# A megakernel on one Trainium2 core: two reorderings on ScalarE, two key copies moved to DMAs, paired maxima, a later projection and PE fillers

## What is computed

```python
# 1: window attention, 8 x 8 windows, 8 heads of 8 channels, rotary q and k
q, k, v = split(xw @ qkv_w.T + qkv_b); q, k = rope2(q), rope2(k)
h = softmax(q * 8 ** -0.5 @ k.T) @ v @ proj_w.T + proj_b
# 2: selective state-space block on layernorm(h), 4096 positions per image, 128 channels, 16 states
xb, z = split(rmsnorm(x) @ in_proj_w.T)
xb = silu(causal_conv4(xb) + conv_b)
delta = softplus(xb @ projDelta_w.T + projDelta_b)
B, C = xb @ projB_w.T, xb @ projC_w.T
s[t] = exp(delta[t] * A) * s[t-1] + xb[t] * delta[t] * B[t]      # 128 x 16 states
h = h + (sum(s * C) + xb * D) * silu(z) @ out_proj_w.T + x       # x is layernorm(h)
# 3: mixture of 6 experts, top 2, on layernorm(h)
w = softmax(top2(softmax(relu(f @ rw1 + rb1) @ rw2 + rb2)))
h = h + sum_e w_e * (relu(relu(f @ w1_e + b1_e) @ w2_e + b2_e) @ w3_e + b3_e)
```

## Time and profile before

| | |
|---|---|
| median of 3 runs | 1665.36 us (1664.95 to 1667.06) |
| the profiled execution's own time | 1668.21 us |
| its span, first to last instruction | 1666.4 us |
| first scan, last scan | 171.5 us, 1599.0 us |
| granted TensorE clock, mean | 0.828 of 2.4 GHz |
| HBM traffic | 274.75 MB read, 20.97 MB written |

### The profile page before, as it was taken

The page is one execution under the profiler, slowest core; times in us unless marked ns, Lnnn a source line. Parts: engine busy times, 40 slices in busy tenths (PEclk is TensorE's granted clock), DMA queues, the critical chain, the costliest instruction groups (busy, mean ns, idle before and its releaser), DMA issues. The chain is left out here.

```text
span 1666.4 us, 25330 instructions
## 1 busy us (share of the span) xinstructions
PE 1186.7 (71%) x7764; PEld 540.7 (32%) x7828; DVE 1251.3 (75%) x1453; ACT 1041.3 (62%) x1973; POOL 1089.3 (65%) x1475
## 2 busy tenths in 40 slices
PE   3665758696868678686968676786869687767565
PEld 1442425151524324151514233241515242212121
DVE  1112787797979788897979697887879797979841
ACT  2335757667585857676675858576776857564521
POOL 2014686777767686777767676777777677777630
PEclk9967968898888889798888888897988887676755
DMA  2002887686868778677868677687768687978720
GB/s 70 6 8 63 217 237 196 193 225 172 230 174 228 183 213 211 194 208 193 224 171 234 175 225 192 205 216 195 207 183 233 173 229 188 252 183 256 214 54 7
DMA packets 205982, 301.62 MB, mean 181 GB/s; under 512 B 70220, under 2 KB 70424, under 8 KB 205720
## 3 DMA queue, kind: packets, MB, share of 16 engines
q1 hardware_dynamic: 205848, 299.99, 66.1%
HBM read 274.75 MB, written 20.97 MB: 177 GB/s over the span
## 5 line engine op out<-in xcount | busy, mean ns | idle before, releaser
L1262 POOL TENSOR_TENSOR hc<-hs,c_rep 128x512 f32<-128x512 f32 x512 | 650.1, 1273 | 244.6 <-DVE hs L1035 244.5
L1035 DVE TENSOR_TENSOR_SCAN hs<-bank,state,xd 128x512 f32<-128x512 f32 x512 | 645.0, 1272 | 63.0 <-issue 44.2
L775 ACT ACTIVATE bank<-dl,a_neg 128x512 f32<-128x512 f32 x512 | 350.8, 688 | 242.1 <-DVE hs L1035 239.1
L1025 DVE TENSOR_TENSOR xd<-xd,bank 128x1024 f32<-128x1024 f32 x256 | 305.8, 1194 | 13.2 <-PE bank L423 7.7
L438 PE MATMUL bank<-hc,wts 128*32 128x512 f32 x1024 | 183.6, 779 | 3.3 <-POOL hc L1262 2.0
L543 PE MATMUL bank<-q_diag,k_heads 128*128 128x128 f32 x1024 | 155.1, 301 | 18.8 <-issue 8.6
L543 PEld LDWEIGHTS bank<-q_diag,k_heads 128*128 128x128 f32 x1024 | 156.3, 218 | 10.9 <-issue 5.0
L1055 DVE TENSOR_REDUCE neg_max<-bank 128x8 f32<-128x512 f32 x128 | 85.7, 675 | 74.3 <-PE bank L531 74.3
L531 PE MATMUL bank<-k_heads,q_diag 64*64 64x512 f32 x512 | 82.2, 715 | 73.2 <-DVE neg_max L1055 43.6
L702 PE MATMUL bank<-e,wts 64*64 64x512 f32 x384 | 70.2, 807 | 86.5 <-ACT e L961 86.5
L599 PE MATMUL bank<-xz,wts 128*128 128x512 f32 x128 | 77.1, 686 | 42.2 <-ACT xz L877 22.0
(11 more groups left out here) (167 smaller groups left out, 2021.2 us busy)
## 6 DMA issues: line engine op xcount, KB each, us to landing
xd<-xdel_rows SPq DMA_DIRECT2D x512, 256.0 KB, 4.5
dl<-delta_rows SPq DMA_DIRECT2D x512, 256.0 KB, 4.1
delta_rows<-delta SPq DMA_DIRECT2D x16, 512.0 KB, 2.9
xdel_rows<-xdel SPq DMA_DIRECT2D x16, 512.0 KB, 3.0
xin<-in_x_dram SPq DMA_DIRECT2D x32, 128.0 KB, 3.0
q_diag<-rot SPq DMA_DIRECT2D x64, 64.0 KB, 3.8
out_dram<-res SPq DMA_DIRECT2D x256, 16.0 KB
wts<-in_packed_dram SPq DMA_DIRECT2D x1, 1528.5 KB, 6.6
```

Of the source, the lines that this page charges most:

```text
L775: act.activation(decay_ps[n % 2][:, :], dl[:, n % 4, :], ACT.Exp, scale=a_neg[:, g:g + 1])\
L1025: dve.tensor_tensor(pair, pair, b_ps[:, :].unsqueeze(1).to_broadcast([128, 2, BAND]), ALU.mult)\
L1035: dve.tensor_tensor_scan(hs[:, n % 4, :], decay_ps[n % 2][:, :], xd[:, n % 8, :], state[:, g:g + 1], ALU.mult, ALU.add).then_inc(scanned.s ...
L1262: pool.tensor_tensor(hc[:, n % 8, :], hs[:, n % 4, :], c_rep[:, BAND * h:BAND * h + BAND], ALU.mult)\
```

## The change

- ACT: Silu with its table loads (slot 9) and Exp and Ln of softplus (slot 13) move into `soften`, called right behind the decay and the values' evacuation in the slot.
- Heads 6 and 7 of `k_heads` are written by 4 DMAs of 16 KB on SP's queue in slot 13, ahead of the queries' in slot 14. ACT copies heads 0 to 5, in slots s = 6 to 8; it has none at s = 5.
- Banks 4 and 5 become one tensor, `both`, and DVE takes the maxima of two windows in one instruction at s = 11, 13, 15, 17. A semaphore of its own, `maxed`, replaces the banks' drained counts for it; PE waits on it ahead of the scores of windows 2, 4, 6 and ahead of the transpose of the maxima.
- The projection's matmul goes from slot 10 to slot 11, ahead of the slot's other matmuls of the experts and of the preparation.
- `keep_busy` issues 3, 3, 3 and 2 bf16 matmuls (zero weights, 512 columns, accumulated into the y bank) at the start of slots 13, 14, 16 and 17.
- The output bias of slot 25 is one matmul of 128 columns instead of two of 64.

```diff
--- before.py
+++ after.py
@@ -81,11 +81,11 @@
-AT = {"S": [10, 12, 14, 16], "max": [10 + _w for _w in range(NW)],
+AT = {"S": [10, 12, 14, 16], "max": [11, 13, 15, 17],
       "T": [19, 20, 22, 23, 25, 26, 28, 29], "P": [21, 21, 24, 24, 27, 27, 30, 30]}
-FILLERS = {}
+FILLERS = {13: 3, 14: 3, 16: 3, 17: 2}
 SOFT = (15, 16, 17, 18, 19, 20, 21, 22)
@@ -104,19 +104,19 @@
 class Use:
-    def __init__(self, bank, filled, drained, index):
-        self.bank, self.index = bank, index
+    def __init__(self, bank, filled, drained, index, before):
+        self.bank, self.index, self.before = bank, index, before
         self.fills, self.drains = filled, drained
         self.filled, self.drained = filled.sem, drained.sem
     def opens(self, chunk):
-        return self.drains.at(chunk, self.index)
+        return self.drains.at(chunk, self.before)
     def full(self, chunk):
         return self.fills.at(chunk, self.index + 1)
     def empty(self, chunk):
-        return self.drains.at(chunk, self.index + 1)
+        return self.drains.at(chunk, self.before + 1)
 def tower(nc, x, packed, select, out):
@@ -130,17 +130,27 @@
         def sig(name, per):
             return Signal(sem(name), per)
-        psum = [ctx.enter_context(nc.psum_tensor(f"bank{i}", [128, 512], F32)) for i in range(8)]
+        psum = [ctx.enter_context(nc.psum_tensor(f"bank{i}", [128, 512], F32)) for i in range(4)]
+        both = ctx.enter_context(nc.psum_tensor("both", [128, 2, 512], F32))
+        psum += [both[:, 0, :], both[:, 1, :]]
+        psum += [ctx.enter_context(nc.psum_tensor(f"bank{i}", [128, 512], F32)) for i in range(6, 8)]
         decay_ps, b_ps, y_ps = psum[0:2], psum[2], psum[3]
-        def bank_uses(stage, uses, first):
-            count = [sum(b == bank for _, b in uses) for bank in range(max(b for _, b in uses) + 1)]
-            signals = [(Signal(sem(f"{stage}_filled{b}"), n), Signal(sem(f"{stage}_drained{b}"), n))
-                       for b, n in enumerate(count)]
-            return {name: Use(psum[first + b], *signals[b], [n for n, x in uses if x == b].index(name))
-                    for name, b in uses}
-
-        A = bank_uses("a", A_USES, 4)
+        def bank_uses(stage, uses, first, apart=()):
+
+            names = [[n for n, b in uses if b == bank] for bank in range(max(b for _, b in uses) + 1)]
+            kept = [[n for n in row if n not in apart] for row in names]
+            signals = [(Signal(sem(f"{stage}_filled{b}"), len(names[b])), Signal(sem(f"{stage}_drained{b}"), len(kept[b])))
+                       for b in range(len(names))]
+
+            def use(name, b):
+                index = names[b].index(name)
+                before = sum(n not in apart for n in names[b][:index])
+                return Use(psum[first + b], *signals[b], index, before)
+
+            return {name: use(name, b) for name, b in uses}
+
+        A = bank_uses("a", A_USES, 4, tuple(f"S{w}" for w in range(NW)))
         Bk = bank_uses("b", B_USES, 6)
         W = bank_uses("w", W_USES, 6)
         G = bank_uses("g", G_USES, 6)
@@ -237,9 +247,10 @@
         x_in = sig("x_in", 32)
         roped = sig("roped", 2)
+        maxed = sig("maxed", NW // 2)
         top_ready = sig("top_ready", 1)
-        heads_in = sig("heads_in", 4 * 16)
-        heads_act = sig("heads_act", HEADS)
+        heads_in = sig("heads_in", 8 * 16)
+        heads_act = sig("heads_act", 6)
         rec_ready = sig("rec_ready", 1)
         att_ready = sig("att_ready", 1)
@@ -329,6 +340,15 @@
                 elif n >= 8 or past(k - 1):
                     sp.wait_ge(scanned.sem, scanned.at(k, n - 7))
                 sp.dma_start(xd[:, n % 8, :], rows_of(xdel_dram, k, group(n), n // NU)).then_inc(xd_in[n % 8].sem, 16)
+
+            def heads(k):
+
+                sp.wait_ge(roped.sem, roped.at(k, 1))
+                for half in range(2):
+                    for h in (6, 7):
+                        p = slice(64 * half + HD * h, 64 * half + HD * h + HD)
+                        sp.dma_start(k_heads[p, :, h, :], rot[p, 1, :].rearrange("p (w j) -> p w j", w=NW))\
+                          .then_inc(heads_in.sem, 16)
             def queries(k):
@@ -367,6 +387,8 @@
                     if has(c + 3):
                         if n == 4:
                             load(c + 3)
+                        if n == 13:
+                            heads(c + 3)
                         if n == 14:
                             queries(c + 3)
                     if has(c + 1):
@@ -469,7 +491,7 @@
                 if s == 18:
                     use = A["top"]
                     fill(use, k)
-                    pe.wait_ge(A["S7"].drained, A["S7"].empty(k))
+                    pe.wait_ge(maxed.sem, maxed.at(k, NW // 2))
                     pe.transpose(use.bank[0:64, 0:128], neg_max[:, :, :], ident).then_inc(use.filled, 1)
             def attend(k, s):
@@ -509,7 +531,8 @@
                     for i in range(4):
                         last = pe.transpose(use.bank[:, 128 * i:128 * i + 128], att[:, 2 * i:2 * i + 2, :], ident)
                     last.then_inc(use.filled, 1)
-                if n == 10:
+            def project_on(k, n):
+                if n == 11:
                     use = O["proj"]
                     fill(use, k)
                     for i in range(4):
@@ -522,9 +545,11 @@
                 uses = A[f"S{w}"], A[f"S{w + 1}"]
                 for use in uses:
                     fill(use, k)
+                if w:
+                    pe.wait_ge(maxed.sem, maxed.at(k, w // 2))
                 if w == 0:
-                    pe.wait_ge(heads_in.sem, heads_in.at(k, 64))
-                    pe.wait_ge(heads_act.sem, heads_act.at(k, HEADS))
+                    pe.wait_ge(heads_in.sem, heads_in.at(k, 128))
+                    pe.wait_ge(heads_act.sem, heads_act.at(k, 6))
                 for odd, use in enumerate(uses):
                     for half in range(2):
                         p, to = slice(64 * half, 64 * half + 64), 64 * (half ^ odd)
@@ -646,9 +671,7 @@
                 if n == 25:
                     use = F["outT"]
                     fill(use, k)
-                    for s in range(2):
-                        pe.matmul(use.bank[64 * s:64 * s + 64, :], eb3_2[:, s, :], wT[0:4 * E, :].bitcast(F32),
-                                  start=True, stop=True)
+                    pe.matmul(use.bank[:, :], eb3_2[:, :, :], wT[0:4 * E, :].bitcast(F32), start=True, stop=True)
                 for e, slot in enumerate((26, 28, 30)):
                     if n == slot:
                         layer3(k, e)
@@ -728,6 +751,8 @@
                         spread_b(c + 1, 1 - odd, 0)
                     if has(k):
                         attend_first(k, s)
+                    if has(c + 2):
+                        project_on(c + 2, n)
                     if has(c - 2):
                         experts(c - 2, SLOTS + n)
                     if has(c - 1) and n == 1:
@@ -871,11 +896,6 @@
                         use = Bk[f"z{h}"]
                         act.wait_ge(use.filled, use.full(k))
                         copy(xz[:, q, 2 + h, :], use.bank[:, :]).then_inc(use.drained, 1)
-                if n == 9:
-                    tables("silu_and_others")
-                    act.wait_ge(Bk["z1"].drained, Bk["z1"].empty(k))
-                    act.activation(xz[:, q, :, :], xz[:, q, :, :], ACT.Silu).then_inc(silu_ready.sem, 1)
-                    tables("natural_log_exp_and_others")
                 for h in range(2):
                     if n == 11 + h:
                         use = Bk[f"d{h}"]
@@ -886,13 +906,20 @@
                             act.wait_ge(kept.sem, kept.at(k - 1, 32))
                         act.activation(delta[:, at], use.bank[:, :], ACT.Relu, bias=col("delta_b"))
                         act.activation(ex_d[:, at], use.bank[:, :], ACT.Abs, bias=col("delta_b")).then_inc(use.drained, 1)
+                if n == 22:
+                    rep(k, "c0", 0)
+
+            def soften(k, q, n):
+                if n == 9:
+                    tables("silu_and_others")
+                    act.wait_ge(Bk["z1"].drained, Bk["z1"].empty(k))
+                    act.activation(xz[:, q, :, :], xz[:, q, :, :], ACT.Silu).then_inc(silu_ready.sem, 1)
+                    tables("natural_log_exp_and_others")
                 if n == 13:
                     act.wait_ge(Bk["d1"].drained, Bk["d1"].empty(k))
                     act.activation(ex_d[:, :], ex_d[:, :], ACT.Exp, scale=-1.0).then_inc(soft_act.sem, 1)
                     act.wait_ge(soft_act.sem, soft_act.at(k, 1))
                     act.activation(ln_d[:, :], ex_d[:, :], ACT.Ln, bias=1.0).then_inc(soft_act.sem, 1)
-                if n == 22:
-                    rep(k, "c0", 0)
             def second(k, q, n):
                 if n == 1:
@@ -966,8 +993,8 @@
             def heads(k, s):
-                if 5 <= s < 9:
-                    for h in (2 * s - 10, 2 * s - 9):
```

(19 more changed lines are left out.)

## The result

The changed kernel takes **1619.26 us** (median of 4 runs, 1617.17 to 1620.35) against 1665.31: a ratio of 0.972, 95% interval 0.9703 to 0.9737. The forecast was 1622 us. The profiled execution took 1618.92 us (span 1617.1; before 1668.21 and 1666.4), so 49.3 us of span went; between the medians it is 46.05.

A forecast was written before the change was run, and what follows sets the result against it. No engine was full, so waits in DVE's in-order queue were taken as the bound. Savings of 36 (chunks 1 to 12), 4.5 (chunks 0, 13, 14), 2 (filling) and 1 (tail), together 43.5 us, gave 1622 us, range 1598 to 1650.

The forecast's parts named there:

- DVE's in-order waits set the chunk: No engine is full; each DVE wait delays the scans behind it, the large ones 9.64 us of a 92.16 us chunk.
- Exp behind the decay: Slot 13: Exp and Ln fit into ACT's wait for the router, ending DVE's 3.75 us wait; the logits come late next.
- Key copies: Two of eight go to DMAs: ACT saves 2 x 0.66 us per chunk, DVE's 0.68 us wait goes; SP's queue 2.6 us, hidden.
- Silu and projection: Around scan 12, one wait replaces another: taken as 0, bounds a gain of 1.04 us and a loss of 1.0.
- Maxima: Paired maxima of 1.2 us, first wait 1.3 us; scan 20 comes 2.9 us earlier, with later pairs 3.0 us per chunk.
- Fillers: Three in slot 13 take PE 0.7 to 1.3 us, two in slot 17 0.8; those of slots 14 and 16 stand in waits.
- Rival B: The clock rises from slot 13 to 18 as PE's idle time shrinks: 4.4 us per chunk, 1601 us; chance 0.22.
- Sum: All terms over the run together save 43.5 us, giving 1622 us for the median.
- Chunks 1 to 12: The twelve chunks with all the work save 3.0 us each: 36 us.
- Chunks 0, 13, 14: These lack the experts or the scores, so half the gain each: 4.5 us.
- Filling: Two key copies fewer on the path in each of three rounds, 0 to 4 us: taken as 2.
- Tail: One output bias matmul for two saves half of 1.90 us on the chain that ended last: 1 us.

The follow-up runs named there:

- experiment 1: The kernel before, with only softplus' Exp and Ln moved directly behind the decay of slot 13: 1636.55 us, ratio 0.985.
- Experiments 4: The changed kernel with softplus' Exp and Ln back at the end of slot 13: 1621.75 us, ratio 0.975.
- 5: The changed kernel with all eight key copies on ACT and no key DMAs: 1620.48 us, ratio 0.975.
- 6: The changed kernel with Exp and Ln back at the end of slot 13 and all eight key copies on ACT: 1646.56 us, ratio 0.990.
- experiment 2: The changed kernel with Silu back at the end of slot 9 and the projection back in slot 10: 1639.60 us, ratio 0.986.
- experiment 3: The changed kernel with Silu kept early but the projection back in slot 10: 1661.76 us, ratio 0.999.
- experiment 7: The changed kernel with one maximum per bank in slots s = 10 to 17 again: 1633.83 us, ratio 0.982.
- experiment 8: The changed kernel without the eleven filler matmuls: 1620.25 us, ratio 0.976.
- experiment 12: The changed kernel with DVE's projection bias sum behind scan 12 and ten more fillers in slots 22, 23 and 24: 1605.91 us, ratio 0.965.
- 9: The kernel before with the eleven filler matmuls alone added: 1661.88 us, ratio 1.000.
- 11: The changed kernel with DVE's projection bias sum moved from the end of slot 11 to behind scan 12: 1615.62 us, ratio 0.972.

## Why the prediction was right, and where not

- **DVE's in-order waits set the chunk.** Right. Of the 3.4 us per chunk 3.0 lie between scan 12 and scan 24 (39.1 us before, 36.1 after); from there to scan 12 of the next chunk it is 53.1 and 52.6 us. Forecast 3.0 in all.
- **Exp behind the decay.** Right in its sign: alone it is worth 25 us (experiment 1). The forecast had 2 us of waiting left for the logits; there are 0.27, since they came at 8.5 us behind scan 12 and not at 10.0. Those 1.5 us are what the B matmul and the sum over states gained by the full clock (2.09 us in place of 3.64), which the forecast left at the low one: of the three low stretches it named only that of slots 16 to 18. Scan 16 was 4.0 us earlier, not 2.5.
- **Key copies.** The step "with slot 13 free of them, the next decay starts at 848.15 instead of 851.4" charged their gain on top of Exp's. Experiments 4 to 6 show that in the whole chunk the two are substitutes: one of them alone gives nearly the whole. At scan 16 they add, as the forecast had them; what absorbs one of them comes later. Of SP's queue the forecast was right: 3.0 us for 2.6, hidden.
- **Silu and projection: "I take 0"** is the step that failed. It is worth 2.1 us a chunk (experiment 2), outside the bounds of -1.0 to 1.04. The step looked at scan 12 alone, where one wait did replace another (1.47 for 1.04, and scan 12 came 0.2 us earlier). What it missed is the logits' way on PE behind scan 12, and the clock there: with the pair in its old place up to 3.5 us of it are at 1.2 GHz, with the pair moved 0.2. It also did not see that, with Silu early, the projection's slot is worth 3.5 us a chunk by itself (experiment 3).
- **Maxima.** Right in size: 1.2 us each, a wait of 1.25 us at the first pair (1.3 forecast), worth 0.010 of the time (experiment 7). But 1.5 us of what scan 20 gained went again by scan 24, which the forecast did not have.
- **Fillers.** Costed as 0.7 to 1.3 us for three; three took 0.81. Rival B came in part, and not by them: between scans 12 and 20 the low clock fell from 13.7 to 6.8 us a chunk, and to 6.8 or 10.2 without the fillers too (experiment 8), while at the end of the chunk it rose from 10.2 to 13.7. The mean went from 0.828 to 0.845. In experiment 12, with fillers in other slots, the stretch at the end is shorter too.
- **Sum.** Chunks 1 to 12: 40 for 36. Chunks 0, 13, 14: 3.5 for 4.5, all of it in chunk 0. Filling: 5.8 for 2; the term looked at the key copies only. Early Silu is not the reason, since without it (experiment 2) the first scan comes at 163.7 us, and with a maximum per bank (experiment 7) at 170.5; what makes up the 5.8 us stays open. Tail: -0.8 for 1; the matmul was priced as two in a row.
- **What was not in the forecast and cost time:** DVE's small instructions, told below, 2 us a chunk.
- **Luck.** That 3.0 us a chunk stands so near 3.4 is in part luck. Scan 20 was early by 4.5 us and not 2.9, through the clock and the logits; 1.5 us of it went again by scan 24. And the parts do not add: undone, Silu and projection cost 2.1 us a chunk, the maxima 1.1, Exp with the key copies 2.7, together more than the 3.4 that all of them bring.

Open: why so many versions come out at the same chunk. The kernel before, experiments 3 and 9 have 92.16 or 92.17; the changed kernel, 5, 8, 11 lie at 88.65 to 88.83, with waits that differ by up to 2 us. In most of them the low-clock stretches stand at the same place in each chunk. Where they do not, they return in a cycle of several chunks: two in 8, three in 7 (90.9, 89.5, 89.2), five in 2. That the clock's pattern holds the length is how I read it; no run took the clock's changes away, so it was not shown.

## What to carry to other kernels

Ask of each moved instruction not only which wait it ends but what else is due at that point of the in-order engine, and what other waits further on can absorb the gain. Here either of two edits could be undone at a cost of 1.6 or 1.1 us at scan 16 and next to nothing in the chunk, and both could not; only runs with each undone, and with both undone, show it. When one engine's copy moves back, the matmul that waits for it must move behind the matmuls that others wait for. Look at the granted clock along the whole path that a change shortens, and again after the change: a forecast that takes it as fixed can miss a part worth 2 us a chunk. Where the clock falls in a repeating pattern, gains can be paid back in the densest stretch. Ten fillers in the waits ahead of a long low stretch helped here, and eleven in slots 13 to 17 did nothing.

## What the runs showed of the hardware

Some DVE instructions that read and write SBUF alone took longer when GpSimd was busy beside them. Softplus' subtraction of one (1024 columns) has a median of 1192 ns after and 694 before; the cast of the weights a mean of 1128 for 605; and an instruction on 8 columns 877 for 207. The last with what ran on GpSimd, in the changed kernel and then in the kernel before:

```profile
836.11 1.28 POOL L1292 TENSOR_TENSOR hc<-hs,c_rep 128x512 f32<-128x512 f32 x1
836.32 1.09 DVE L1192 TENSOR_SCALAR st_f<-st_f 128x8 f32<-128x8 f32 x1
```

```profile
869.27 1.27 POOL L1262 TENSOR_TENSOR hc<-hs,c_rep 128x512 f32<-128x512 f32 x1
...
870.94 0.16 DVE L1162 TENSOR_SCALAR st_f<-st_f 128x8 f32<-128x8 f32 x1
```

It ends at 837.41, with GpSimd's multiplication (836.11 + 1.28 = 837.39). Before the change the same instruction came 0.40 us behind the end of that multiplication. Not all are touched: the reciprocals of 8 columns took 0.19 us beside GpSimd's work too. With another instruction on 8 columns (592 ns for 227) these are four groups, and they add 32.5 us over the run, which is why DVE's busy time rose. The subtraction's 7.6 us come with early Exp: before, both engines stood idle for the same softplus wait, and in experiments 6 and 9, where Exp is late, it takes 694 ns again. The other 24.9 us come with the paired maxima, which shift DVE's list against GpSimd's: the instruction on 8 columns has a mean of 0.86 to 0.88 us in all ten kernels with pairs and 0.21 to 0.23 in the four without (before, 1, 7, 9), and from scan 20 to scan 24 it is 12.4 us in the changed kernel and 10.9 in 7. No kernel with pairs and these instructions in another place was run. The Trainium skill, "SBUF — State Buffer", section "SBUF: two separate sides", names a port pair that VectorE and GpSimd share; it is locked for a whole instruction, and the loser blocks. The trace agrees for these instructions: 1.09 us for 8 columns, ended by the other engine's end.
